# A causal attention of 16 heads before two expert layers and a linear attention: the loop over head pairs written out, value products of two key groups in one run, scores of two key chunks in one run, the mask as rounded fp32 tiles

## The reference

```python
K = jnp.einsum('bpd,ihd->biph', x, W_K)
Q = jnp.einsum('bpd,ihd->biph', x, W_Q)
V = jnp.einsum('bpd,ihd->biph', x, W_V)
scores = jnp.einsum('biph,biqh->biqp', K, Q)
mask = jnp.tril(jnp.ones((q_len, q_len), dtype=bool))
scores = jnp.where(mask[None, None, :, :], scores, NEG_INF)
attn = jax.nn.softmax(scores / np.sqrt(d_head).astype(np.float32), axis=-1)
z = jnp.einsum('biph,biqp->biqh', V, attn)
z_flat = jnp.transpose(z, (0, 2, 1, 3)).reshape(b, q_len, -1)
out = jnp.einsum('bqf,df->bqd', z_flat, W_O)
...
x = x + _L0_attn_a_ref(_layernorm(x, axis=-1), ...)
x = x + _L0_ffn_ref(_layernorm(x, axis=-1), ...)
x = x + _L0_attn_b_ref(_layernorm(x, axis=-1), ...)
x = x + _L0_ffn_ref(_layernorm(x, axis=-1), ...)
```

## Time and profile before

| | us |
|---|---|
| time, median of 3 runs | 1457.94 |
| lowest and highest | 1456.09 and 1460.14 |
| profiled execution: span | 1455.8 |
| PE busy in the span | 1256.4 |
| DVE busy | 963.7 |
| ACT busy | 793.8 |
| attention, from the first projection at about 20 to about 1130 | 1110 |

### The profile page before, as it was taken

The page is one execution under the profiler, slowest core; times in us unless marked ns, Lnnn a source line. Parts: engine busy times, 40 slices in busy tenths (PEclk is TensorE's granted clock), DMA queues, the critical chain, the costliest instruction groups (busy, mean ns, idle before and its releaser), DMA issues. The chain is left out here.

```text
span 1455.8 us, 25494 instructions
## 1 busy us (share of the span) xinstructions
PE 1256.4 (86%) x7936; PEld 866.7 (60%) x7936; DVE 963.7 (66%) x2284; ACT 793.8 (55%) x2146; POOL 149.0 (10%) x190
## 2 busy tenths in 40 slices
PE   5999899989998998999899989999997194886376
PEld 3666666666656665666666666656665193443275
DVE  5776577668756775776577668757774264798344
ACT  6766466656665665666466656666663063232143
POOL 1000000000000000000000000000000443554343
PEclk9999999999999999999999999999998596898588
DMA  4940200020002002000200020001000121000023
GB/s 107 157 101 1 61 1 1 1 60 1 2 15 46 1 1 60 1 1 1 61 1 1 1 60 1 2 15 44 1 1 1 37 62 56 1 0 0 21 59 96
DMA packets 52731, 41.62 MB, mean 29 GB/s; under 512 B 14177, under 2 KB 41442, under 8 KB 52578
## 3 DMA queue, kind: packets, MB, share of 16 engines
q1 hardware_dynamic: 50018, 34.50, 11.0%
q0 software_dynamic: 2560, 5.26, 1.1%
HBM read 13.49 MB, written 9.48 MB: 16 GB/s over the span
## 5 line engine op out<-in xcount | busy, mean ns | idle before, releaser
L278 DVE TENSOR_REDUCE at_cmax<-at_ps 128x1 f32<-128x512 f32 (+3 forms) x576 | 350.3, 620 | 167.9 <-PE at_ps L454 166.4
L371 ACT ACTIVATE at_prob<-at_ps,at_nmax 128x512 f32<-128x512 f32 (+3 forms) x640 | 391.4, 621 | 88.1 <-DVE at_nmax L281 53.7
L464 PE MATMUL at_ps<-ident,at_prob 128*128 128x128 f32 x2176 | 309.0, 276 | 20.8 <-DVE at_probT L287 11.5
L451 PE MATMUL at_ps<-at_k_st,at_q_parts 128*128 128x512 f32 (+3 forms) x640 | 289.3, 452 | 31.2 <-issue 22.8
L464 PEld LDWEIGHTS at_ps<-ident,at_prob 128*128 128x128 f32 x2176 | 251.2, 141 | 94.8 <-issue 25.9
L481 PE MATMUL at_ps<-at_probT,at_v 128*64 128x256 f32 (+1 forms) x2304 | 295.0, 379 | 3.8 <-DVE at_probT L287 3.2
L378 ACT ACTIVATE at_probT<-at_ps 128x512 f32<-128x512 f32 (+1 forms) x288 | 165.2, 573 | 236.5 <-PE at_ps L464 234.9
L454 PE MATMUL at_ps<-at_k_st,at_q_parts 128*128 128x512 f32 (+3 forms) x640 | 258.1, 405 | 0.0
L287 DVE COPY at_probT<-at_ps 128x512 f32<-128x512 f32 (+1 forms) x288 | 189.6, 658 | 69.0 <-PE at_ps L464 66.6
L481 PEld LDWEIGHTS at_ps<-at_probT,at_v 128*64 128x64 f32 x2304 | 141.7, 136 | 129.6 <-issue 51.2
L451 PEld LDWEIGHTS at_ps<-at_k_st,at_q_parts 128*128 128x128 f32 x640 | 125.1, 196 | 111.7 <-ACT at_prob L371 59.3
(11 more groups left out here) (186 smaller groups left out, 1279.3 us busy)
## 6 DMA issues: line engine op xcount, KB each, us to landing
at_q_parts<-at_q_parts SPq DMA_DIRECT2D x64, 256.0 KB, 4.0
f_xs<-slots_in SPq DMA_DIRECT2D x48, 64.5 KB
slots_in<-zeros SPq DMA_DIRECT2D x2, 1536.0 KB, 17.9
wall<-in_L_ffn_w_dram SPq DMA_DIRECT2D x1, 2048.0 KB, 17.5
wall<-in_L_ffn_w_dram SPq DMA_DIRECT2D x4, 512.0 KB, 6.2
f_got<-slots_out SPq DMA_DIRECT2D x8, 256.0 KB, 3.6
out_dram<-x SPq DMA_DIRECT2D x4, 256.0 KB, 2.4
slots_out<-f_ys,f_back POOLq DMA_INDIRECT x48
```

Source lines behind the costliest of these rows:

```text
L278: dve.tensor_reduce(cmax[:, u % SLOTS, c:c + 1], bank, AX.X, ALU.max).then_inc(s_cmax, 1)
L371: act.activation(prob[j % 2][u % 4][:, c * BANK:c * BANK + w], ring[k % RING][:, 0:w], ACT.Exp, bias=nmax[:, u % SLOTS:u % SLOTS + 1], acc ...
L451: pe.matmul(bank[:, 0:w], q_hi[h][:, r * P:(r + 1) * P], keys, start=True, stop=False)
L464: last = pe.transpose(turn_ps[h][:, b * P:(b + 1) * P], prob[j % 2][2 * i + h][:, t * P:(t + 1) * P], ident[:, :])
```

## The change

The diff, cut to its core:

```diff
@@ issue_order and back_of @@
-            if g:
-                items += [("value", j, g - 1), None]
-        return items + [("value", j, j), None, ("leave", j)]
+            if g and g % 2 == 0:
+                items += [("value", j, (g - 2, g - 1)), None, None, None]
+        return items + [("value", j, (j,) if j % 2 == 0 else (j - 1, j)), None, ("leave", j)]
...
-            for k in range(max(ns, ne)):
-                if k < ns:
-                    order.append(("score", w, k))
+            for k in range(0, max(ns, ne), 2):
+                slots = range(k, min(k + 2, max(ns, ne)))
+                order += [("score", w, c) for c in slots if c < ns]
                 if opens and k == 0:
                     order.append(("sums", j))
-                order += fill.pop(0) if fill else []
-                order += dealt.pop(0) if w > 4 else []
                 order += [("exp", w - 1, c) for c in range(ne) if exp_slot(c, ne) == k]
+                for i in slots:
+                    order += fill.pop(0) if fill else []
+                    order += dealt.pop(0) if w > 4 else []
+                order += [("exp", w - 1, c) for c in range(ne) if exp_slot(c, ne) == k + 1]
@@ buffers @@
-        wq_fix, wk_fix = sb("wq_fix", [D, P]), sb("wk_fix", [D, P])
-        prob = [[sb(f"prob{k}{i}", [P, T - P * (i < 2)]) for i in range(4)] for k in range(2)]
+        prob = [[sb(f"prob{k}{i}", [P, T - P * (i < 2) - 2 * P * (k == 0)]) for i in range(4)] for k in range(2)]
-        probT = [[sb(f"probT{h}{k}", [P, BANK]) for k in range(2)] for h in range(2)]
+        probT = [[sb(f"probT{h}{k}", [P, BANK]) for k in range(TURNED)] for h in range(2)]
-        identb = sb("identb", [P, P], BF16)
-        maskb = sb("maskb", [P, P], BF16)
+        identr = sb("identr", [P, P], F32R)
+        maskr = sb("maskr", [P, P], F32R)
@@ on every engine @@
-                with pe.Fori(0, PAIRS - 1) as pair:
+                for pair in range(PAIRS - 1):
                     run(order, pair, pair + 1, False)
@@ tensor @@
-                                pe.matmul(bank[:, w - P:w], identb[:, :], maskb[:, :], start=False, stop=False)
+                                pe.matmul(bank[:, w - P:w], identr[:, :], maskr[:, :], start=False, stop=False)
...
-                                pe.wait_ge(s_probT[h], N_GR * pair + n + 2)
+                                pe.wait_ge(s_probT[h], N_GR * pair + first_group[j] + run_of[-1] + 2)
...
-                            if i == 0:
-                                pe.wait_ge(s_wfix, made + 1)
-                            pe.matmul(ring[(N_SC + i) % RING][:, :], (wk_fix, wq_fix)[kind][:, :], xnT[:, c * BANK:(c + 1) * BANK],
+                            pe.matmul(ring[(N_SC + i) % RING][:, :], wT["kq"[kind]][:, made, :], xnT[:, c * BANK:(c + 1) * BANK],
```

More of the change, by code:

```diff
@@ L233, in _ @@
                 make_identity(pool, ident[:, :], s_c0, s_const)
-                make_identity(pool, identb[:, :], s_c1, s_const)
-                pool.memset(maskb[:, :], 0.0).then_inc(s_c2, 1)
+                pool.wait_ge(s_const, 1)
+                pool.tensor_copy(identr[:, :], ident[:, :]).then_inc(s_const, 1)
+                maskf = probT[0][0][:, 0:P]
+                pool.memset(maskf, 0.0).then_inc(s_c1, 1)
+                pool.wait_ge(s_c1, 1)
+                pool.affine_select(out=maskf, in_=maskf, compare_op=ALU.is_ge, fill=MASKED, base=0,
+                                   pattern=[[-1, P]], channel_multiplier=1).then_inc(s_c2, 1)
                 pool.wait_ge(s_c2, 1)
-                pool.affine_select(out=maskb[:, :], in_=maskb[:, :], compare_op=ALU.is_ge, fill=MASKED, base=0,
-                                   pattern=[[-1, P]], channel_multiplier=1).then_inc(s_const, 1)
+                pool.tensor_copy(maskr[:, :], maskf).then_inc(s_const, 1)
                 pool.memset(wo_bd[:, :, :, :], 0.0).then_inc(s_const, 1)
[L240 to L250, removed]
             @block.vector
@@ L334, in _ @@
                 run(opening, 0, 0)
-                with dve.Fori(0, PAIRS - 1) as pair:
+                for pair in range(PAIRS - 1):
                     run(order, pair, pair + 1)
@@ L377, in run @@
                             act.wait_ge(s_turn[0], N_GR * pair + n + 1)
[L378 removed]
+                            act.activation(probT[0][n % TURNED][:, 0:w], turn_ps[0][:, 0:w], ACT.Copy).then_inc(s_probT[0], 1)
                         elif it[0] == "leave":
@@ L402, in _ @@
                 run(opening, 0, 0)
-                with act.Fori(0, PAIRS - 1) as pair:
+                for pair in range(PAIRS - 1):
                     run(order, pair, pair + 1)
@@ L467, in run @@
                         elif it[0] == "value":
[L468 to L469 removed]
+                            _, j, run_of = it
                             if j == 0:
                                 pe.wait_ge(s_v, N_V * made)
[L472 removed]
+                            if run_of[0] == 0:
                                 pe.wait_ge(s_acc2, STEPS * pair + j + 1)
                             for h in range(2):
[L475 to L483 removed]
+                                pe.wait_ge(s_probT[h], N_GR * pair + first_group[j] + run_of[-1] + 2)
+                            for g in run_of:
+                                n = first_group[j] + g
+                                for h, b in ((0, 0), (1, 0), (1, 1), (0, 1)):
+                                    t = 2 * g + b
+                                    last_tile = t == 2 * j + 1
+                                    to, w = (P, P) if last_tile else (0, 2 * P)
+                                    rows = slice(DH * h, DH * (h + 1))
+                                    last = pe.matmul(z_ps[rows, to:to + w], v[:, t, rows], probT[h][n % TURNED][:, 2 * P * b:2 * P * b + w],
+                                                     start=t == 0, stop=last_tile)
+                            if run_of[-1] == j:
                                 last.then_inc(s_z, 1)
```

16 lines of the change are left out of this document (4 added, 12 removed).

## The result

The changed kernel takes 1500.88 us (median of 4 runs, 1500.65 to 1501.15) against 1458.3 for the kernel before beside it; the ratio is 1.0291 [1.0277, 1.0306]. The forecast was 1472, its range ended at 1492. The direction was right, and the size was off by a factor of three.

A forecast was written before the change was run, and what follows sets the result against it. PE was taken to bound the attention (busy 1042 of 1110 us), tied to DVE and ACT by a ring of five banks. The terms -36 - 40 + 2 + 88 gave +14 on a median of 1457.94, so 1472 us, range 1443 to 1492.

The forecast's parts named there:

- The loop, -36: Six jumps back between pairs: writing out removes 23.8 us of issue gaps and 12.5 of slow clock.
- The value runs, -40: Value products on PE: 15 fewer runs a pair at 0.33 each, 4.9 a pair, 40 us saved over 8 pairs.
- the mask, +2: Mask product in 256 chunks: slower fp32 weight loads, mostly hidden, cost 2 us, bounds 0 and +26.
- The waits of the new order, +88: PE in the attention: 14.2 us of new waits a pair less 3.0 that go, net +11.2, 9.5 in pair 8.
- the wait of the earlier trace: An existing PE wait of 0.9, taken as now covered by two scores; part of the 3.0 a pair that goes.
- the ring: Five banks: scores wait for an exponential queued behind a transpose's copy; four times 1.03, twice 0.6, 5.3 a pair.
- value runs behind their own transposes: Last runs in quads 1, 3, 5, 7 wait for DVE's copy; 1.0 for three of them, 3.1 a pair.
- projections: Transpose copies queue behind ACT's two copies per projection; three times 1.1 and 0.1 more, 3.4 a pair.
- third transposes: Same head transposed again with only the other head's transposes between, waiting for the copy; five places, 2.4 a pair.
- More waits than counted: Rival: each 1 us more of waits a pair adds 8 us; at 17 new a pair 1496 us; chance 0.08.
- Waits largely covered: Rival: new waits come to three quarters (1445 us) or half (1417 us) of those counted; chance 0.25.
- writing out brings nothing: Rival: issue gaps come with each new stretch of code, not the jump, and stay; 1508 us; chance 0.05.

The follow-up runs named there:

- written out: Kernel before with only the pair loop written out (single scores, one value group per run, bf16 mask): 1417.78 us, ratio 0.972.
- + paired scores: Written-out kernel with the scores of two key chunks in one run, value groups still one by one: 1440.17 us, ratio 0.987.
- + value edit: Written-out kernel with value products of two groups per run, transposes dealt to new slots, three buffers for turned groups, single scores: 1481.05 us, ratio 1.0159.
- + crowded places, runs split: Kernel with two-group value runs, its pushed-together transposes left in place, each merged run split again: 1447.98 us, ratio 0.9928.
- + merges, places kept: Written-out kernel, transposes in their old slots, first of each two value runs moved down to the second, 15 merges a pair: 1418.58 us, ratio 0.9726.
- all parts, places kept: Changed kernel with all four parts, but transposes in their former slots and merged runs at their second group's place: 1433.44 us, ratio 0.9837.
- seven merges, four moves: Written-out kernel with seven value-run merges a pair and four items moved (transposes, two exponentials, projection 2): 1397.17 us, ratio 0.9585.

## Why the prediction failed, by its own steps

The numbers below are start-to-start times of PE's matmuls, the median over pairs 2 to 7. The fastest twentieth of the matmuls with the same neighbours, over all twelve kernels, is taken as their time without a wait; their sum over a pair is the stream. What a start-to-start is over that, where it is over 0.08, is a wait. The rest, 3.4 to 4.2 a pair, is small everywhere.

| kernel | pair | stream | waits | time |
|---|---|---|---|---|
| written out | 130.2 | 120.9 | 5.6 | 1417.8 |
| + paired scores | 132.7 | 120.0 | 9.3 | 1440.2 |
| + value edit | 138.1 | 116.3 | 17.8 | 1481.1 |
| + crowded places, runs split | 134.0 | 120.6 | 9.7 | 1448.0 |
| + merges, places kept | 130.3 | 116.1 | 10.5 | 1418.6 |
| all parts, places kept | 131.8 | 115.6 | 12.7 | 1433.4 |
| the changed kernel | 140.4 | 116.1 | 20.1 | 1500.9 |
| seven merges, four moves | 127.4 | 118.9 | 4.8 | 1397.2 |

*The loop, -36:* right in its two parts; -39.4 on the spans, 3 of them from waits inside the loop that the forecast had looked for only in pair 8.

*The value runs, -40, and the mask, +2:* right. The changed kernel's stream is 4.8 a pair shorter than the written-out one's (7 x 4.82 + 4.87 = 38.6 us) where these two terms gave 38. That paired scores save nothing by themselves was off by 0.9 a pair.

*The waits of the new order, +88:* this is the step that failed. Measured against the written-out kernel they are 7 x 15.05 + 14.6 = 120 us (the small rest, 0.5 in a pair and 0.9 in pair 8, included), of which 1.6 in pair 8 are the slow clock; so 118 us of waits, and 4.8 for the clock with the 3.2 of pairs 1 and 4. The places were right but for one (the wait of the earlier trace rows, taken as gone, stays at 0.46), and the sizes were low in every kind, a pair: the ring 6.2 for 5.3, value runs behind their own transposes 3.6 for 3.1 (1.20, 1.04, 1.35), projections 3.6 for 3.4 (1.20, 1.20, 1.21), third transposes 3.7 for 2.4 (0.52, 0.88, 0.91, 0.60, 0.41 and small ones); and gone 2.6 for 3.0. Together 14.5 for 11.2. In pair 8 it was 13.0 for 9.5, the clock left out: against pair 8 of the written-out kernel PE's idle time before scores goes from 0.9 to 4.5, before value runs from 0.4 to 4.6, before transposes from 5.1 to 8.2. The account: 30.4 us of waits too few and 4.8 of clock, less 3.4 of the loop and 0.6 of the stream, are 31, against 43.6 - 14 = 29.6 on the spans; the other 1.6 lie before the first score and behind the attention.

Three things made the sum larger. First, a score that waits straight behind another score has a restart behind it: its second product starts 0.11 later than without (6 x 0.11 of the ring's 0.9). Second, the forecast took most links from places where the queue ahead of them was empty, and in the crowded order it is not. Pair 3 of the changed kernel, third transposes of quad 4, head 0, its PE, ACT and DVE:

```profile
364.83 1.35 PE L458 MATMUL at_ps<-ident,at_prob 128*128 128x128 f32 x8
366.89 0.66 PE L458 MATMUL at_ps<-ident,at_prob 128*128 128x128 f32 x4 [0.71 <-ACT at_probT L372]
...
364.90 0.69 ACT L365 ACTIVATE at_prob<-at_ps,at_nmax 128x512 f32<-128x512 f32 x1 [0.66 <-DVE at_nmax L275]
365.49 0.19 ACT L365 ACTIVATION_READ_ACCUMULATOR at_prob<-at_ps,at_nmax 128x1 f32 x1
365.58 0.68 ACT L365 ACTIVATE at_prob<-at_ps,at_nmax 128x512 f32<-128x512 f32 x1
366.15 0.20 ACT L365 ACTIVATION_READ_ACCUMULATOR at_prob<-at_ps,at_nmax 128x1 f32 x1
366.24 0.59 ACT L372 ACTIVATE at_probT<-at_ps 128x512 f32<-128x512 f32 x1
```

The transposes start at 364.83, and the copy not 0.64 later, as in the earlier trace rows, but 1.41 later (366.24): two exponentials stand ahead of it, and the first of them had waited for DVE until 364.90. PE waits 0.88 from start to start for it, where a copy alone gives the forecast's 0.3 to 0.4. (Which of its five sizes the forecast gave to this place it does not say.)

Here is another, the last value run of quad 5:

```profile
401.85 0.50 PE L445 MATMUL at_ps<-at_k_st,at_q_parts 128*128 128x512 f32 x1 [0.99 <-ACT at_prob L365]
402.18 0.39 PE L448 MATMUL at_ps<-at_k_st,at_q_parts 128*128 128x512 f32 x1
402.41 0.49 PE L458 MATMUL at_ps<-ident,at_prob 128*128 128x128 f32 x3
404.18 0.65 PE L476 MATMUL at_ps<-at_probT,at_v 128*64 128x256 f32 x4 [1.28 <-DVE at_probT L281]
...
402.61 0.69 DVE L272 TENSOR_REDUCE at_cmax<-at_ps 128x1 f32<-128x512 f32 x1 [1.03 <-PE at_ps L448]
403.22 0.16 DVE L289 TENSOR_REDUCE at_rsum<-at_esum 128x4 f32<-128x16 f32 x1
403.41 0.18 DVE L291 RECIPROCAL at_rinv<-at_rsum 128x4 f32<-128x4 f32 x1
403.51 0.53 DVE L281 COPY at_probT<-at_ps 128x384 f32<-128x384 f32 x1
```

DVE had stood idle for 1.03 while PE itself waited (0.99 at 401.85, so the score's second product, L448, came late), then had a reduction and the row sums to do before the copy. So one wait does lengthen the next: the forecast's sentence that DVE and ACT catch up while PE stands is wrong where they stand idle for PE's late product. With places kept PE stands 4.3 us before value runs in place of 39.3, so DVE and ACT with the same work do keep up there.

Third, the clock. During the last value run of quad 5 in pairs 1 and 4 the windows above show it at 0.54 and 0.58, mostly at the lower of the two levels (1.2 GHz), after PE had stood for 1.28; the two pairs are 1.6 us longer each. The last run of quad 1 in pair 8 is the third such place (0.53), behind stands of 1.08 and 1.13, and costs another 1.6:

```profile
1034.46 0.55 PE L458 MATMUL at_ps<-ident,at_prob 128*128 128x128 f32 x3 [1.08 <-DVE at_probT L281]
1036.14 2.98 PE L476 MATMUL at_ps<-at_probT,at_v 128*64 128x256 f32 x16 [1.13 <-DVE at_probT L281]
```

The forecast had no term for it. Pair 3 has the stand of 1.28 as well (404.18 above) and keeps the full clock (1.00 in pair 3's window), so what decides it stays open.

*The rivals.* "More waits than counted" is what happened, and its price of 8 us for each microsecond a pair holds. The new waits are 17.1 a pair (6.2 + 3.6 + 3.6 + 3.7), where its example has 17 and 1496 us. It had a chance of 0.08 and should have had more. "Waits largely covered" and "writing out brings nothing" are refuted, the latter by 41 us.

Some sums of the forecast are off by 2 us by its own terms: three quarters of the waits give 1445 and not 1443, 17 new a pair 1494 and not 1496, and 16.5 give 1490 and not 1492. None of it bears on the outcome.

What the forecast never did is to ask which line of the change makes the waits. It took the merges as a saving and the order's new places as given. The dealing of the value groups, by its empty places (`None`) and the place of the run, is an edit of its own, and taken back alone it gives 67 us.

Open: why two transposes a pair wait 0.15 longer in the loop, which half of the crowded places costs more, what decides the clock, and whether the crowded order's loss in quad 7 is its projections' places or its transposes', since both kernels that keep the places move both.

## What to carry to other kernels

In a written-out order of items for three engines, value the place of each item and the joining of items as separate edits: joining runs in place cost nothing net here and paid 13 us where the trace showed no new wait behind the join, while pushing the transposes into one bank together, with the run that needs them straight behind, cost 67 us. When the chains of a new order are priced from an old trace, price each with what stands ahead of it in the other engines' queues and not alone. Write out a loop over seven long bodies if there is room: 41 us of 1458, for nothing else changed.

## What the runs showed of the hardware

A score that stands straight behind another score and waits for its PSUM bank pays about 0.11 us more at its second product (from the start of the first product to that of the second 0.33 in place of 0.23 at a chunk of 512; six such waits a pair in the changed kernel). Behind transposes the first product takes 0.31 in any case, and the wait adds 0.02 (the written-out kernel, two waits of 0.7 a pair). Sixteen value products in one run instead of two of eight save 0.31 to 0.32 (4.6 and 4.8 by 15), crowded or not. And fp32 weights for the mask, which raise the loads' busy time by 19 us in the attention, cost nothing in time (0.3 us between the two medians), as each load lies beside another product.
